# Two exchanges of order at the entry of the expert layers: down projection before gate and up, routing before the low part

## The reference, cut to what matters

```
router_logits = x @ gate_w                       # 1024 x 64 experts
probs = softmax(router_logits)
top_vals, top_idx = top_k(probs, 8); top_vals /= sum(top_vals)
rw[t, top_idx] = top_vals                        # all other weights 0
g = einsum('th,ehi->tei', x, w_gate)             # 64 experts, 96 inner columns
u = einsum('th,ehi->tei', x, w_up)
h = silu(g) * u * rw[:, :, None]
out = einsum('tei,eih->th', h, w_down)
```

## Time and profile before

| what | us |
|---|---|
| median of 3 runs | 2032.64 |
| lowest, highest | 2025.01, 2032.80 |
| the profiled execution: its time | 2025.01 |
| the profiled execution: its span | 2023.1 |
| TensorE busy in the span | 1846.3 (91%) |
| VectorE, ScalarE, GpSimd busy | 1069.1, 910.3, 685.5 |

### The profile page before, as it was taken

One profiled execution on the slowest core, in us unless ns is written; L12 is line 12 of the kernel. 1 busy time (PEld: TensorE's weight loads), 2 busy tenths in 40 slices (PEclk: granted clock), 3 DMA queues, 4 the chain that ended last, 5 costly groups with the idle time before them and its releaser, 6 DMA issues. The chain is left out here.

```text
span 2023.1 us, 30362 instructions
## 1 busy us (share of the span) xinstructions
PE 1846.3 (91%) x10596; PEld 1268.7 (63%) x10603; DVE 1069.1 (53%) x1804; ACT 910.3 (45%) x1909; POOL 685.5 (34%) x609
## 2 busy tenths in 40 slices
PE   6899899999998998999999986999984789999997
PEld 3333688888885555788888863333263367777775
DVE  6775444444445654444444466888344345555533
ACT  3577333333334664333333333788811145555521
POOL 5100366666653102666666643000000233223200
PEclk8899999999999999999999998999986599999998
DMA  4300444444421302544444404500005000000000
GB/s 127 84 1 1 131 111 116 111 111 111 110 54 43 91 2 68 145 112 111 109 109 109 112 1 109 62 1 1 1 0 122 0 1 1 2 1 1 1 1 21
DMA packets 136840, 121.71 MB, mean 60 GB/s; under 512 B 84290, under 2 KB 122650, under 8 KB 136570
## 3 DMA queue, kind: packets, MB, share of 16 engines
q1 hardware_dynamic: 136729, 120.24, 23.7%
HBM read 111.41 MB, written 8.65 MB: 59 GB/s over the span
## 5 line engine op out<-in xcount | busy, mean ns | idle before, releaser
L1355 DVE TENSOR_TENSOR e_inner_lo<-e_inner,e_inner_hi 128x512 fp32r<-128x512 f32 x192 | 247.3, 1288 | 390.2 <-ACT e_inner_hi L1324 390.1
L1343 POOL TENSOR_TENSOR e_wsilu<-e_silu,e_rw 128x512 f32<-128x512 f32 x192 | 261.4, 1362 | 225.8 <-ACT e_silu L1318 163.9
L1294 PE MATMUL psum<-e_x_hi,e_w_hi 128*128 128x512 f32 x768 | 303.6, 395 | 8.6 <-DVE e_inner L1363 6.5
L1294 PE MATMUL psum<-e_x_hi,e_w_lo 128*128 128x512 f32 x768 | 299.2, 390 | 0.0
L1294 PE MATMUL psum<-e_x_lo,e_w_hi 128*128 128x512 f32 x768 | 299.1, 390 | 0.0
L1318 ACT ACTIVATE e_silu<-psum 128x512 f32<-128x512 f32 x192 | 114.7, 597 | 345.1 <-PE psum L1294 345.1
L1350 POOL TENSOR_TENSOR e_w_lo<-e_raw,e_w_hi 128x384 fp32r<-128x384 f32 x180 | 221.1, 1228 | 127.9 <-ACT e_w_hi L1331 114.6
L1294 PEld LDWEIGHTS psum<-e_x_hi,e_w_hi 128*128 128x128 f32 x768 | 144.3, 188 | 50.2 <-DVE e_inner L1363 16.7
L1050 DVE TENSOR_REDUCE c_mx<-psum 128x1 f32<-128x1024 f32 x128 | 150.7, 1219 | 28.6 <-PE psum L924 28.1
L1294 PEld LDWEIGHTS psum<-e_x_hi,e_w_lo 128*128 128x128 f32 x768 | 144.3, 188 | 30.6
L1294 PEld LDWEIGHTS psum<-e_x_lo,e_w_hi 128*128 128x128 f32 x768 | 144.4, 188 | 28.8
(11 more groups left out here) (356 smaller groups left out, 3318.0 us busy)
## 6 DMA issues: line engine op xcount, KB each, us to landing
e_rw<-e_rw_dram SPq DMA_DIRECT2D x60, 384.0 KB, 5.1
e_rw<-e_rw_dram SPq DMA_DIRECT2D x60, 256.0 KB, 5.3
e_raw<-in_L_ffn_w_gate SPq DMA_DIRECT2D x64, 192.0 KB, 2.6
e_raw<-in_L_ffn_w_up SPq DMA_DIRECT2D x64, 192.0 KB, 2.5
e_raw<-in_L_ffn_w_down SPq DMA_DIRECT2D x32, 384.0 KB, 3.7
e_rw<-e_rw_dram SPq DMA_DIRECT2D x68, 128.0 KB, 4.8
c_parts_dram<-c_part SPq DMA_DIRECT2D x8, 384.0 KB, 2.5
a_qs<-a_parts_dram SPq DMA_DIRECT2D x42, 64.0 KB, 2.3
```

The lines of the kernel that those rows point to most:

```text
L1294: last = nc.tensor.matmul(bank[u % 2][:], self.w[a][s][:, KC * which + k, j * P:(j + 1) * P], self.x[b][:, k, h * HALF:(h + 1) * HALF], st ...
L1343: self.core.nc.gpsimd.tensor_tensor(self.wsilu[:, u % 2, :], self.silu[:, u % 2, :], self.rw[s][:, j, h * HALF:(h + 1) * HALF], ALU.mult). ...
L1355: self.core.nc.vector.tensor_tensor(self.inner_parts[1][:, u % 3, :], self.inner[:, u % 2, :], self.inner_parts[0][:, u % 3, :], ALU.subtr ...
```

## The change

It makes two exchanges of neighbours, each in both expert layers, once per layer. TensorE runs the first `down` (unit 0) before `gate_up` of unit 2 and no longer behind it; VectorE runs the second half's `route_begin` before `low_inner` of unit 0 and no longer behind it. No instruction is added or removed.

```
@@ layer_of_tensor
         moe.logits(pe, r, 1, 6)
+        moe.down(pe, first, 0, first=True)
         moe.gate_up(pe, r, first, 2)
-        moe.down(pe, first, 0, first=True)
         moe.down(pe, first, 1)
         moe.turn_rows(pe, r, 1, 7)
@@ layer_of_vector
         moe.multiply(dve, first, 0)
+        moe.route_begin(dve, r, 1, 6)
         moe.low_inner(dve, first, 0)
-        moe.route_begin(dve, r, 1, 6)
         moe.multiply(dve, first, 1)
         moe.low_inner(dve, first, 1)
         moe.route_end(dve, r, 1)
```

## The result

The median is 2043.82 us over 6 runs (2039.18 to 2046.94), against 2032.72 over 6 runs of the kernel before. The ratio is 1.0057 with a 95% interval of 1.0043 to 1.0072: 11.1 us slower, where 5.3 was forecast and 2043.0 was the range's upper end. The same kernel, timed again beside 29 runs of the kernel before, gave 2043.49 against 2033.0, ratio 1.0051 (1.0038 to 1.0063), 10.5 us.

What follows compares the result with a forecast made beforehand. TensorE alone paces an expert layer's loop, so its entry, set by the second half's routing, decides. Delays of 2.86 us (second layer) and 2.4 (first) sum to 5.3, median 2037.9 us (+0.26%); range 2028.0 to 2043.0.

Steps and rivals of the forecast that it cites:

- The pause behind the logits: TensorE, second layer: waits 2.0 us between the logits and `down(0)`, which needs `low_inner(0)`.
- `low_inner(0)` held up by GpSimd's `low_weights(1)`: VectorE, second layer: `low_inner(0)` ends 0.55 us behind `low_weights(1)`, at 792.79 and not 791.72.
- `activate(2)` late and `high_inner(1)` with it: ScalarE, second layer: `activate(2)` starts 797.26, before 794.28; `high_inner(1)` follows 0.49 us later; `low_inner(1)` ends 2.86 us late.
- the second pause: TensorE, second layer: about 2.7 us before `down(1)` in place of the 1.90.
- `route_exp` early to no use: Second layer: the routing's start 0.76 us earlier only adds to a slack of 3.9 us and earns nothing.
- the loop dense behind it: Steady part of an expert layer: TensorE busy 99.31 of 100 us, so a delay at the entry is not made up.
- the middle of 1.96 and 2.85: First layer's delay, 2.4 us: 2.85 if GpSimd's `low_weights(1)` goes first, 1.96 if VectorE's `low_inner(0)` does.
- a rival at 0.14: TensorE's clock falls at the new pauses: +1.4 to 2.7 us per layer, 2040.7 half hit, 2043.3 wholly; chance 0.14.
- in the second layer 1.90 us cost no clock: TensorE, kernel before: a 1.90 us pause brought no clock fall, so not every pause does; the first layer's 2.38 did.
- the routing going earlier: Rival: `route_exp` sets the chain, so the earlier routing start gains 1.5 us over both layers, 2031.1; chance 0.05.
- absorption: Rival: TensorE has slack before `gate_up(5)`, so the delay is hidden and the time is 2032.6; chance 0.05.
- the other mix of executions: Rival: the changed kernel's median falls with the fast execution and reads 2030.3 with the same mechanism; chance 0.17.

Runs made afterwards that it cites:

- TensorE's exchange alone: Kernel before with only `down` of unit 0 moved ahead of `gate_up` of unit 2, VectorE in its old order: 2040.41 us, ratio to before 1.0033.
- the filled one: Changed kernel plus 8 matmuls, results thrown away, on TensorE between the logits and `down` of unit 0: 2039.94 us, ratio to before 1.0028.
- VectorE's exchange alone: Kernel before with only `route_begin` moved ahead of `low_inner` of unit 0, TensorE in its old order: 2035.43 us, ratio to before 1.0008.
- before, ScalarE exchanged: Kernel before with only ScalarE's `high_inner` of unit 1 moved ahead of `activate` of unit 2: 2034.97 us, ratio to before 0.9999.

## Why the prediction was wrong

**The forecast of the order held, step by step.** The pause behind the logits (2.0 forecast, 1.97), `low_inner(0)` held up by GpSimd's `low_weights(1)`, `activate(2)` late and `high_inner(1)` with it, the second pause (2.7, 2.58), `route_exp` early to no use, the loop dense behind it. In the first layer, where I took 2.4 as the middle of 1.96 and 2.85, GpSimd came first in each of the three profiles, yet the delay by the order was 2.4 and not 2.85: `low_inner(1)` moved from 6.51 to 10.46 us behind the logits, 3.95, of which 1.58 are the clock. GpSimd's `low_weights(1)` ended 1.33 behind the logits, where the forecast of the upper end had 1.89. That the middle came out is luck: which engine is first was one question, and when GpSimd gets there, which I had carried over from one profile, another. In the second layer it happened both ways. In the changed kernel's second profile VectorE was first, `low_inner(0)` took 0.68 and the pause only 1.62:

```profile
800.24 0.68 DVE L1355 TENSOR_TENSOR e_inner_lo<-e_inner,e_inner_hi 128x512 fp32r<-128x512 f32 x1
```

```profile
800.26 1.52 POOL L1350 TENSOR_TENSOR e_w_lo<-e_raw,e_w_hi 128x384 fp32r<-128x384 f32 x1
```

The Trainium skill ("SBUF — State Buffer", "Who interferes with whom") calls the port pair an exclusive lock. The traces agree in this: whichever of the two started first kept its short duration (0.99 for GpSimd, 0.68 for VectorE), and the other was stretched (1.03 and 1.52). But it does not follow, as I had it, that only two totals are possible.

**The term that was left out is the clock.** The sum priced `down(0)` and `gate_up(2)` at full clock, 1.49 + 2.88, and so put the clock at nothing. They took 5.98 us in the second layer of the first profile and 5.96 in the first, 1.6 more each. From the earlier trace rows to the changed rows `low_inner(1)` moved by 4.44 us against the logits, 2.86 by the order and 1.58 by the clock. 5.3 + 2 x 1.6 = 8.5, and the profiles' entries say 8.15. Over the three profiles of each kernel `low_inner(1)` ends 6.41 and 10.35 us behind the logits (means of six), 3.95 later: 2.37 by the order, 1.58 by the clock, 7.9 in both layers.

I had this as a rival at 0.14, with a price of 1.4 to 2.7 per layer. The measured 1.6 lies in it, but partly by luck: the price was worked out for `gate_up(2)` alone, and of the 1.6 us, 1.1 fell on `down(0)` and 0.5 on `gate_up(2)`. The chance was the wrong one: all six profiled entries of the changed kernel have the slow burst (these two groups of matmuls at half clock) in them. From `low_inner(0)`'s end to `low_inner(1)`'s it is 8.55 to 8.60 us in each, as in the first layer of TensorE's exchange alone (8.56), and 6.98 and 6.99 where the clock held, in that kernel's second layer and in both layers of the filled one (6.99 and 6.98).

The step that failed is "in the second layer 1.90 us cost no clock", taken as evidence that such pauses are mostly free. It was one execution; in two later profiles of the same kernel the clock fell in that layer too.

And a fall costs little where the burst behind it is `turn_rows` (0.44 us by the prediction's own rows), nothing at `gate_up(5)` where it is `down(2)` and `gate_up(4)` and the routing rows are still on their way, and 1.6 us where the burst is on the chain to `activate(2)`. The six entries of before have five falls between the logits and `gate_up(5)`, two over `turn_rows` and three over `down(2)` and `gate_up(4)`. The six of the changed kernel have eleven: one over `down(0)` and `gate_up(2)` in each, and one more over `down(2)` and `gate_up(4)` in five of them. The change put a fall where it counts, and did not take away those beside the path. The rule of the Trainium skill that I cited ("TensorE: Matmul & The Clock Gate", "What's actually happening"), that activity releases the throttle, was the right one to weigh more.

**The baseline.** That the first profile of before lay 7.6 under the median was carried over rightly: most of it is in other stages.

**What stays open.** 8.15 us of the loss are placed, and the profiled executions bear it out: 2041.44, 2043.14 and 2040.46 us for the changed kernel (mean 2041.7), 2033.56 and 2033.64 for the second and third of before, 8.1 between them. The medians over all runs differ by 10.5 to 11.1. The changed kernel's profiled executions lie 2 us under its median, those of before at theirs. The stage between the expert layers was 1.5 us longer in the changed kernel (means of three 172.1 and 170.6), but it varies from 169.7 to 173.4 over all kernels. Over all 30 executions of the changed kernel on record and all 92 of the kernel before, the medians are 2043.0 and 2033.3 and the means 9.9 apart, so the part not placed is nearer 2 us than 3. No run here tells whether it is that stage's clock or something the profiles don't catch.

The other rivals: the routing going earlier (1.5 us gain) failed with VectorE's exchange alone; absorption failed, as the loop stays at 361 us; the other mix of executions did not occur, the lowest of all 30 executions of the changed kernel being 2037.6.

## What to carry to other kernels

When two neighbours on one engine change places, follow what the later of them feeds through the in-order lists of the other engines: here ScalarE's list handed TensorE's delay to an independent chain, and one exchange there undid the whole loss, though the clock still fell. In this kernel a new pause on TensorE had to be priced with a slow burst behind it wherever that burst was on the path, and could go at nothing only where it wasn't. And one profile shows one draw of the clock; where a term rests on "it didn't fall here", a second profile is worth more than a finer sum.

## What the runs showed of the hardware

- TensorE's clock fell to half behind pauses of 1.10 us (TensorE's exchange alone, first layer), 1.98 (changed) and 2.38 (before), and during one of 3.12 (before, ScalarE exchanged). It held behind others of 0.90 (TensorE's exchange alone, second layer), 1.90 and 2.88 (before) and 2.98 (VectorE's exchange alone). At the same place of the kernel before, ahead of `down(1)` in the first layer, it fell behind 1.83 us in the second profile and held behind 1.85 in the third. So in these runs the last pause's length alone does not tell. Matmuls whose results are thrown away, put into a pause, took 3.5 to 3.9 us off the changed kernel's median.
- The way of the routing rows from `copy_rows` through DRAM to `weigh(3)` took from 8.5 to 10.5 us with the same DMAs, 8.5 to 9.5 in the kernel before alone. The spread of 2 us over all kernels is as much as the gain of most of the reorderings tried here.
- `low_inner` (VectorE) takes 0.68 to 0.69 us alone. Where it lasted longer, in 241 of 243 cases around the entries of all fourteen profiles, it ended 0.53 to 0.57 us behind the end of an instruction of GpSimd that ran beside it; the longest took 1.82 (before, ScalarE exchanged, second layer).
